# X's diagonal blocks written to memory once per unit instead of once per half

## The reference

```python
A = -(jnp.einsum('bhnid,bhnjd->bhnij', k_beta, kc) * decay) * strict
Tm = jax.scipy.linalg.solve_triangular(eye - A, jnp.broadcast_to(eye, A.shape), lower=True, unit_diagonal=True)
u = jnp.einsum('bhnij,bhnjv->bhniv', Tm, v_beta)
kcd = jnp.einsum('bhnij,bhnjd->bhnid', Tm, k_beta * jnp.exp(gc)[..., None])
```

## Time and profile before

| | |
|---|---|
| median of three runs | 4329.88 us (4328.74 to 4330.48) |
| the profiled execution | 4325.86 us |
| its span | 4324.1 us, mean granted clock 0.99 |
| TensorE (PE) busy | 4169.7 us, 96% |
| DVE busy | 3618.1 us, 84% |
| POOL busy | 3028.6 us, 70% |
| ACT busy | 2590.9 us, 60% |
| transfers of the kernel's own queue | 31.9% of 16 DMA engines' span |
| xb<-X | 512 transfers of 32 KB |

### The profile page before, as it was taken

The page is one execution under the profiler, slowest core; times in us unless marked ns, Lnnn a source line. Parts: engine busy times, 40 slices in busy tenths (PEclk is TensorE's granted clock), DMA queues, the critical chain, the costliest instruction groups (busy, mean ns, idle before and its releaser), DMA issues. The chain is left out here.

```text
span 4324.1 us, 91678 instructions
## 1 busy us (share of the span) xinstructions
PE 4169.7 (96%) x29748; PEld 3124.3 (72%) x29748; DVE 3618.1 (84%) x7996; ACT 2590.9 (60%) x5686; POOL 3028.6 (70%) x8986
## 2 busy tenths in 40 slices
PE   4899999999999999999999999999999999998998
PEld 2577777777777777777777777777777777776665
DVE  6788888888888888888888888888888888888454
ACT  3566666666666666666666666666666666665311
POOL 1777777777777777777777777777777777776231
PEclk8899999999999999999999999999999999999999
DMA  5333323333333333333333233333343333322110
GB/s 154 74 77 81 90 65 83 81 90 74 77 89 90 80 73 77 89 89 74 80 95 87 65 84 81 90 69 93 78 102 74 77 80 86 90 64 72 35 49 25
DMA packets 879055, 343.73 MB, mean 79 GB/s; under 512 B 742384, under 2 KB 828144, under 8 KB 869360
## 3 DMA queue, kind: packets, MB, share of 16 engines
q1 hardware_dynamic: 878576, 337.86, 31.9%
HBM read 256.87 MB, written 80.86 MB: 78 GB/s over the span
## 5 line engine op out<-in xcount | busy, mean ns | idle before, releaser
L1061 DVE SCALAR_TENSOR_TENSOR CV<-pp,CW,CV 128x1023 f32<-128x1023 f32 (+2 forms) x768 | 979.2, 1275 | 18.9 <-ACT CV L1717 12.1
L450 PE MATMUL pp<-A,W 128*128 128x512 f32 x2048 | 973.9, 599 | 15.0 <-DVE CV L1061 9.5
L2193 POOL TENSOR_TENSOR UL<-UL,TM 128x126 f32<-128x126 f32 (+22 forms) x1984 | 735.0, 370 | 155.4
L2190 POOL TENSOR_TENSOR TM<-UL,XL 128x126 f32<-128x126 f32 (+22 forms) x1984 | 701.7, 354 | 152.3 <-issue 12.5
L1817 ACT ACTIVATE VS<-qa,EB 128x128 f32<-128x128 f32 x1024 | 319.4, 365 | 471.6 <-PE qa L577 471.5
L1204 DVE SCALAR_TENSOR_TENSOR St<-St,TAB,kv 128x128 f32<-128x128 f32 x1024 | 309.8, 344 | 347.6 <-PE kv L587 342.6
L450 PEld LDWEIGHTS pp<-A,W 128*128 128x128 f32 x2048 | 368.6, 193 | 284.4 <-issue 266.6
L631 PE MATMUL emit<-Wo,NTr 128*128 128x256 f32 x2048 | 496.5, 385 | 1.6 <-ACT NTr L1850 1.6
L610 PE MATMUL emit<-Wz,A 128*128 128x256 f32 x2048 | 494.6, 384 | 0.0
L631 PEld LDWEIGHTS emit<-Wo,NTr 128*128 128x128 f32 x2048 | 373.7, 190 | 91.0 <-issue 29.7
L1806 ACT ACTIVATE QE<-qa,TAB 128x128 f32<-128x128 f32 x1024 | 316.7, 361 | 195.7 <-PE qa L567 194.2
(11 more groups left out here) (309 smaller groups left out, 8807.3 us busy)
## 6 DMA issues: line engine op xcount, KB each, us to landing
GB<-gcd SPq DMA_DIRECT2D x64, 1024.0 KB, 5.6
W<-wqkv SPq DMA_DIRECT2D x256, 128.0 KB, 3.8
kb<-TB SPq DMA_DIRECT2D x256, 128.0 KB
XL<-xb SPq DMA_DIRECT2D x128, 256.0 KB, 4.0
K<-kb SPq DMA_DIRECT2D x64, 512.0 KB, 4.8
UL<-c_u SPq DMA_DIRECT2D x64, 256.0 KB, 2.9
xb<-X SPq DMA_DIRECT2D x512, 32.0 KB, 1.6
Wz<-wz SPq DMA_DIRECT2D x64, 256.0 KB, 4.6
```

The lines of the kernel that those rows point to most:

```text
L450: ins = t.matmul(bk.pp[:, 512 * h:512 * h + 512], m.W[:, c, k, :], m.xnT[:, w // KH % 2, c, 512 * h:512 * h + 512], start=c == 0, stop=c == 1)
L1061: v.scalar_tensor_tensor(m.CV[:, t, d:S], bk.pp[:, 0:S - d], m.CW[:, w % KH, t, 3 - d:4 - d], m.CV[:, t, d:S], ALU.mult, ALU.add).then_inc ...
L2190: gp.tensor_tensor(m.TM[:, 0:a, 0:b], m.UL[:, 0:a, k:k + 1].to_broadcast([128, a, b]), m.XL[:, k, k + 1:32].unsqueeze(1).to_broadcast([128 ...
L2193: gp.tensor_tensor(m.UL[:, 0:a, k + 1:32], m.UL[:, 0:a, k + 1:32], m.TM[:, 0:a, 0:b], ALU.subtract).then_inc(s["sub"], 1)
```

## The change

`xo` loses its argument h. It waits until all of X is made (`4 * w + 4`) and writes both halves with four transfers, each of 32 partitions x 16 matrices x 32 floats. In the lead-in and in the loop it stands where `xo(w, 1)` stood; the place of `xo(w, 0)` falls empty. The counts that `xl` and `egw` wait for go from 128 to 64 a unit. No buffer changes.

```diff
-    def xo(w, h):
+    def xo(w):
         if not inside(w):
             return
-        sp.wait_ge(s["x"], 4 * w + 2 * h + 2)
+        sp.wait_ge(s["x"], 4 * w + 4)
         sp.wait_ge(s["dxl"], 32 * w)
         for i in range(4):
-            q.dma_start(dr.xb[i, 8 * h:8 * h + 8].rearrange("u a b -> a u b"),
-                        m.X[w % 2][32 * i:32 * i + 32, 8 * h:8 * h + 8, 32 * i:32 * i + 32]).then_inc(s["dxo"], 16)
+            q.dma_start(dr.xb[i].rearrange("u a b -> a u b"),
+                        m.X[w % 2][32 * i:32 * i + 32, :, 32 * i:32 * i + 32]).then_inc(s["dxo"], 16)
...
-        sp.wait_ge(s["dxo"], 128 * (w + 1))
+        sp.wait_ge(s["dxo"], 64 * (w + 1))
...
-            sp.wait_ge(s["dxo"], 128 * (NU - 1))
+            sp.wait_ge(s["dxo"], 64 * (NU - 1))
...
         ldw(1, 2)
-        xo(0, 0)
         index(1)
-        xo(0, 1)
+        xo(0)
...
         kto(1)
-        xo(1, 0)
         index(2)
         ldw(2, 3)
         ldx(3)
-        xo(1, 1)
+        xo(1)
...
         kti(2)
-        xo(2, 0)
         ldw(3, 2)
-        xo(2, 1)
+        xo(2)
...
             ui(u + 2)
-            xo(u + 2, 0)
             ldw(u + 3, 2)
             kto(u + 2)
-            xo(u + 2, 1)
+            xo(u + 2)
             xl(u + 2)
```

## The result

The changed kernel takes 4333.42 us (4328.65 to 4337.97, 22 runs) against 4326.51 (4320.54 to 4330.48, 22 runs) for the kernel before, timed in turns: a ratio of 1.0017, 95% interval 1.0011 to 1.0023, so some 7 us slower. A second set of runs gave 1.0013 (1.0005 to 1.0022). That is within the 0.2% drawn as the line for "no change that can be told", though both intervals leave out 1, so the sign of the loss is clear. The profiled execution took 4332.28 us, 6.4 more than that of the kernel before, and its span is 4330.5.

A forecast was written before the change was run, and what follows sets the result against it. TensorE was taken to bound the kernel at 61.09 us a unit; +5.3 (late units) and +0.2 (start) made +5.5 us, 4331.4 on the profiled execution, 4335 on the runs' scale. Range 4321 to 4354, no change that can be told.

The forecast's parts named there:

- What is removed: On SP's queue, four of eight xb issues a unit go, under SP's idle time: gain 0 in the steady state.
- what moves: On SP's queue, ldw(u+3, 2) and kto(u+2) start some 4 us earlier; their readers come late, so worth 0.
- the feared collision of kb with N1: Rival: kb's early writes hold up N1's reads if these need over 5.2 us; 4348 or 4353, chance 0.08.
- What gets larger: The remaining xb group carries both halves, 64 KB an issue, and lands later: +0.6 us on XL in every unit.
- Who feels it: At POOL's substitution behind XL: ordinary units cover the delay and lose nothing; the late units lose 5.3 us in all.
- the cover of 0.9 us: Between XL and L1150 by way of POOL: a normal unit absorbs some 0.9 us of lateness without loss.
- The ten late units: Units 4, 9, ... 49, where an xb issue stalls, have no cover left: 0.53 us each, +5.3 us.
- the factor of 0.88: Share of XL's lateness passed to L1150, from unit 34: 1.05 us lost over XL's 1.19 us.
- The step that failed: On SP, the transfers queued behind xl, ldw among them, were each for a use many us away: 0.
- The sign TensorE would have shown: If the forecast was right, TensorE's matmuls would wait some 13 us for L1152.
- The start: In the first units, -0.4 from an earlier first XL and +0.6 in unit 1, paced by POOL: +0.2 us.
- the stalls leave the critical issues: Rival: fewer SP issues break the every-fifth stall pattern; up to -11.3 us, 4319; chance 0.14, 0.10 of it beyond the line.

The follow-up runs named there:

- the order by itself: Kernel before with ldw(u+3, 2) and kto(u+2) put ahead of xo(u+2, 0), both halves still written apart: 4328.24 us against 4330.97, ratio 1.0001.
- the shifted kernel: Kernel before with 20 tiny matmuls put ahead of TensorE's first transpose: 4324.45 us against 4324.86, ratio 1.0002.
- the second dose: Against the kernel before: both halves in eight 32 KB transfers behind the last X quarter, ldw(u+3, 0) moved behind kto(u+2): 4412.82 us, ratio 1.0202.
- the doses: Against the kernel before: eight 32 KB transfers behind the last X quarter, W's first quarter in place (4444.74 us) or moved ahead (4412.82 us).
- the repeat: The changed kernel measured once more beside the kernel before: 4331.47 us against 4324.86, ratio 1.0013.
- an edit of TensorE's list: Changed kernel with 20 tiny matmuls put ahead of TensorE's first transpose: 4328.90 us against 4326.90, ratio 1.0004.
- the split: Kernel before, reordered, 12 of 16 matrices written behind the third X quarter, 4 behind the fourth: 4324.55 us; with 20 tiny matmuls on TensorE 4318.35.

## Why the prediction was right, and where not

The time and its size were right: 5.1 us over the median was said, 6.9 came. The main idea held as well: XL goes out later, ordinary units cover it, late units pay. The parts stand differently, and the sum owes something to luck.

*What is removed, what moves*: 0 and 0. Right; the order by itself is 1.0001, and the feared collision of kb with N1 isn't there. But 4.95 us was not the slowest read of N1: unit 29 took 5.8, with a code packet in it. The Trainium skill (DMA: Bandwidth & Descriptors, Rules for kernel authors) has small transfers better coalesced. Per byte this trace agrees, with 64 KB landed in 2.0 us and 32 KB in 1.6; but on the path stood the landing of one transfer, and that grew.

*What gets larger*: +0.6 us on XL was taken from ub's row; 0.42 was measured. N1's landing of 2.3 us, a read, was too long a guide for a write, 2.0.

*Who feels it*, the ordinary units: right, nearly all at 61.09, and the cover of 0.9 us was near. A lateness of 1.1 cost unit 47 nothing in the shifted kernel, and at the second dose 0.8 of 1.97 was covered. What the reading from unit 32 missed is that POOL's lateness has other exits than L1150: at the doses it came out at `ty`, and beside it W's way left only 0.5.

*The ten late units*: 0.53 each was predicted, 5.3 in all. They lost 12.2 us instead of 9.5, 0.27 each (11.8 in the profile of the repeat): the term was sized at twice its value. XL's 0.42 us instead of 0.6 is a part of it. The larger part is the factor of 0.88, which laid unit 34's whole loss to XL's 1.19. With a cover of 0.9, XL alone would have cost 0.3 (an estimate); the rest came with N1's slow read. In the changed kernel POOL started 0.55 us later in these ten units, near what was predicted, but N1's read took 4.4 us on average instead of 5.0, so that less came through. In the repeat it took 4.9.

*The step that failed*: "Queued behind xl on SP are ldw, kti, ldw, ldz, ldt, ldg, each for a use many us away: 0." The second ldw is W's first quarter, wanted 4.3 us after its issue in unit 7. With the stall that in units 7, 12, 17, 22, 27 and 59 now falls on XL's issues, these units lose 0.36 to 0.58 us each, 2.7 in all, where none did before. The size is uncertain: in the profile of the repeat the same six lose 1.2, and two of them (12 and 22) nothing in spite of the stall. The sum came out near because one term was twice too large, this one was missing, and 1.6 us of the difference between the two profiles fall behind unit 61, of which the prediction said nothing. The sign TensorE would have shown, some 13 us of waits for L1152, was 4.7 (7.0 in the repeat).

*The start*: +0.2 predicted, -0.2 measured. XL went 1.5 us earlier, as worked out (94.30). Neither can be told from nothing, since unit 3 moves by some us from one execution to the next.

*The rival "the stalls leave the critical issues"*: the pattern didn't break with four issues fewer, since it isn't SP's. It took an edit of TensorE's list to break it. The loop then shrank by 9.7 us with the split and by 8.7 without, near the price of 11.3, but in the times 6.5 us came of it with the split and nothing measurable without.

## What to carry to other kernels

When transfers are merged, look at what is written behind the event that the reader waits for, not at their count: merging a half that had gone out early with the half that the reader waits for puts its bytes on the path. Follow every transfer queued behind the delayed one to its own reader before calling it free, by issue time and first use. When a late unit is used to price a delay, look for everything else that was late in it; here two stalls that alone cost at most some tenths of a us cost 1 us together. A lateness that returns at a fixed count of units, with an instruction packet in each, can be moved by a few instructions more at the head of the list whose code it is, here TensorE's. And a split of some us between stages, read from one profile each, needs a second profile before it is believed.

## What the runs showed of the hardware

A 16 KB instruction packet that started inside a group of four issues lengthened them on SP by 0.8 to 1.6 us (3.23 instead of 1.95 in unit 34), though the code was another engine's. A read of N1 with such a packet in it took up to 5.8 us to land instead of 3.8. Four writes of 512 pieces of 128 B landed in 2.0 us each, four of 256 in 1.6. And a delay of 1.97 us in one transfer lengthened units without a stall by 1.47 us, in a kernel whose TensorE is 96% busy.
